# First attention with a constant guard and scores issued ahead of the transposes; expert weights read eight slots later

## The reference

```python
x = x + L0_xattn(layernorm(x), ctx, ctx, mask, Wq, bq, Wk, bk, Wv, bv)   # softmax attention over 257 rows
x = x + L0_attn(layernorm(x), ...)                                       # time mix and channel mix
x = x + L0_ffn(layernorm(x), Wg, We, be)                                 # 8 experts, top 2
x = x + L1_xattn(layernorm(x), ctx, wq, wk, wv, wo, ...)                 # quantised linear layers on ctx
x = x + L1_attn(layernorm(x), ...)                                       # state-space scan
x = x + L1_ffn(layernorm(x), gate_w, ..., w1, b1, w2, b2)                # 8 experts, top 1
```

```python
xn = ctx * rsqrt(mean(square(ctx), -1) + 1e-6)
scale = 127.0 / maximum(max(abs(xn), -1), 1e-5)
xq = round(xn * scale)
```

## Time and profile before

| | |
|---|---|
| median of 3 runs | 2150.19 us (2148.49 to 2154.41) |
| the profiled execution's own time | 2157.34 us |
| its span, first to last instruction | 2155.6 us |
| PE busy | 1442.8 us, 67% |
| DVE busy | 1382.0 us, 64% |
| ACT busy | 988.5 us, 46% |
| POOL busy | 750.6 us, 35% |
| mean granted TensorE clock | 0.773 of full speed |
| loop of the first attention | about 104 to 272 us of the span |
| the last two blocks | about 1380 us to the end |

### The profile page before, as it was taken

How to read it: one execution, slowest core, us unless ns; L and a number is a source line. 1 busy time by engine, 2 the same in 40 slices (tenths; PEclk the granted TensorE clock), 3 DMA queues, 4 the chain that set the end, 5 groups by cost and what they waited for, 6 DMA issues and landing times. The chain is left out here.

```text
span 2155.6 us, 34484 instructions
## 1 busy us (share of the span) xinstructions
PE 1442.8 (67%) x12500; PEld 798.0 (37%) x12500; DVE 1382.0 (64%) x2466; ACT 988.5 (46%) x1792; POOL 750.6 (35%) x804
## 2 busy tenths in 40 slices
PE   5578833336766498148888359344539879879998
PEld 3334412224544343025655133100114434434666
DVE  1267677773334676837777774399899889889110
ACT  2288722222111253225556233433339868868454
POOL 0034300000000532133344000056568688688543
PEclk8556666667888599569899579655659989989999
DMA  1245300001001053265564123599656546534000
GB/s 69 107 181 209 136 20 0 0 0 44 0 0 37 2 194 135 46 117 90 95 102 77 29 79 110 124 231 225 161 115 151 127 98 154 130 88 108 1 11 10
DMA packets 147472, 194.81 MB, mean 90 GB/s; under 512 B 106527, under 2 KB 111583, under 8 KB 134272
## 3 DMA queue, kind: packets, MB, share of 16 engines
q1 hardware_dynamic: 147332, 192.92, 35.4%
HBM read 146.46 MB, written 23.36 MB: 79 GB/s over the span
## 5 line engine op out<-in xcount | busy, mean ns | idle before, releaser
L2453 POOL TENSOR_TENSOR mf_st<-mf_st,mf_c_rep 128x1024 f32<-128x1024 f32 x128 | 300.9, 2351 | 348.4 <-DVE mf_st L2527 348.3
L2527 DVE TENSOR_TENSOR_SCAN mf_st<-mf_dA,mf_u_ps 128x512 f32<-128x512 f32 x256 | 310.4, 1213 | 0.0
L2355 PE MATMUL mf_y_ps<-mf_st,c_consts 128*32 128x512 f32 x512 | 155.8, 798 | 180.3 <-POOL mf_st L2453 133.4
L2638 ACT ACTIVATE mf_dA<-c_dt,c_neg_a 128x496 f32<-128x496 f32 x256 | 167.1, 701 | 116.1 <-DVE mf_st L2527 115.6
L2397 PE MATMUL mf_eh<-mf_parts,mf_w 128*128 128x512 f16 x768 | 198.1, 397 | 18.5 <-POOL mf_parts L2476 11.1
L2521 DVE TENSOR_TENSOR mf_u_ps<-mf_st,mf_b_ps 128x512 f32<-128x512 f32 x256 | 177.8, 695 | 25.7 <-DMA mf_st<-xs 14.7
L2417 PE MATMUL mf_ey<-mf_w,mf_hid 128*128 128x256 f16 x1536 | 192.9, 277 | 0.0
L2480 POOL TENSOR_TENSOR mf_hid<-mf_g,mf_hid 128x512 f16<-128x512 f32 x128 | 148.8, 1163 | 98.6 <-ACT mf_g L2655 98.5
L2417 PEld LDWEIGHTS mf_ey<-mf_w,mf_hid 128*128 128x128 f16 x1536 | 152.5, 99 | 49.9 <-issue 6.0
L1073 POOL TENSOR_SCALAR mg_we<-mg_we 128x2048 f32<-128x2048 f32 x2 | 10.8, 5395 | 432.3 <-DMA mg_we<-in_l_we 432.3
L2652 ACT ACTIVATE mf_hid<-mf_eh,c_vecs 128x512 f16<-128x512 f32 x128 | 88.0, 687 | 112.6 <-PE mf_eh L2397 112.1
(11 more groups left out here) (476 smaller groups left out, 2944.0 us busy)
## 6 DMA issues: line engine op xcount, KB each, us to landing
mf_st<-xs SPq DMA_DIRECT2D x64, 1024.0 KB, 7.2
a_ctx_t<-in_ctx_t SPq DMA_DIRECT2D x16, 1024.0 KB, 6.6
a_ctx_n<-in_ctx_n SPq DMA_DIRECT2D x16, 1024.0 KB, 4.9
mo_raw<-in_l_w SPq DMA_DIRECT2D x16, 512.0 KB, 3.7
ws<-mo_split SPq DMA_DIRECT2D x32, 256.0 KB, 2.4
mf_w<-ws SPq DMA_DIRECT2D x32, 256.0 KB, 14.6
xs<-mi_xc SPq DMA_DIRECT2D x16, 256.0 KB, 4.1
zs<-mi_sz SPq DMA_DIRECT2D x4, 1024.0 KB, 6.8
```

Of the source, the lines that this page charges most:

```text
L2355: m = e.matmul(y_ps[T * j:T * j + T, :], c.pick[:, gg, :], st[u % RING][:, j, :], start=(gg == 0), stop=(gg == 3))
L2453: e.tensor_tensor(half(u, h), half(u, h), over(c_rep[u // UNITS % 2][:, :], [P, 2, BT], 1), ALU.mult).then_inc(hcs("done"), 1)
L2527: e.tensor_tensor_scan(st[u % RING][:, j, :], dA[:, n % AHEAD, :], u_ps[j % 2][:, :], 0.0, ALU.mult, ALU.add).then_inc(hs("done"), 1)
L2638: e.activation(by_batch(dA[:, n % AHEAD, :])[:, :, 1:], dt, ACT.Exp, scale=c.neg_a[:, at:at + 1]).then_inc(dAs("done"), 1)
```

## The change

In the first attention the guard under the maximum becomes the constant `LEAST` in place of the root of the mean square: `roots` is gone with its two activations, the squares add straight into `c.c_ss` and the maxima are written straight to `c.c_max`, so that both copies go. On PE `score(t+1)` now stands ahead of `turn(t)`. In the last two blocks the expert matrices are read in slots 8 to 23.

```diff
+LEAST = 1e-5 * RMS_EPS ** 0.5
...
-        scale = Steps(sem("scale"), ["keep_max", "keep_ss", "guard", "flip", "scale"], 2)
+        scale = Steps(sem("scale"), ["guard", "flip", "scale"], 2)
...
             def turns(t, u, n):
-                turn(t, u)
                 if not last(t):
                     score(t + 1, 1 - u, n + u)
+                turn(t, u)
                 if not first(t):
                     turn_out(t - 1, 1 - u)
                 weigh(t, u, n)
...
-                e.tensor_reduce(qs[u][:, :], ctx_n[u][:, :, :, :].rearrange("p b k c -> p (b k) c"), AX.X, ALU.max,
+                e.tensor_reduce(c.c_max[:, bass.ds(t * 2 * BPT, 2 * BPT)], ctx_n[u][:, :, :, :].rearrange("p b k c -> p (b k) c"), AX.X, ALU.max,
                                 apply_absolute_value=True).then_inc(absmax("done"), 1)
...
                 e.wait_ge(*absmax.at("done", t))
-                e.tensor_copy(c.c_max[:, bass.ds(t * 2 * BPT, 2 * BPT)], qs[u][:, :]).then_inc(scale("keep_max"), 1)
-                e.wait_ge(*root_s.at("root", t))
-                e.tensor_copy(c.c_ss[:, bass.ds(t * 2 * BPT, 2 * BPT)], ss[u][:, :]).then_inc(scale("keep_ss"), 1)
-                e.wait_ge(*scale.at("keep_ss", t))
-                e.tensor_tensor(qs[u][:, :], qs[u][:, :], root[u][:, :], ALU.max).then_inc(scale("guard"), 1)
+                e.wait_ge(*roundings.at("done", t - 2))
+                e.tensor_scalar(qs[u][:, :], c.c_max[:, bass.ds(t * 2 * BPT, 2 * BPT)], LEAST, None, ALU.max).then_inc(scale("guard"), 1)
...
                 e.wait_ge(n_loaded[u], n * 16)
-                e.wait_ge(*scale.at("keep_ss", t - 2))
                 for r in range(2 * BPT):
                     e.wait_ge(*(squares.at("done", t, r - 1) if r else squares.at("done", t - 1)))
                     e.activation(sq[:, :], ctx_n[u][:, r // 2, r % 2, :], ACT.Square,
-                                 accum_out=ss[u][:, r:r + 1]).then_inc(squares("done"), 1)
-
-            def roots(t, u):
-                e.wait_ge(*squares.at("done", t))
-                e.wait_ge(*scale.at("guard", t - 2))
-                e.activation(root[u][:, :], ss[u][:, :], ACT.Ln, scale=1.0 / C,
-                             bias=c.eps[:, 1:2]).then_inc(root_s("log"), 1)
-                e.wait_ge(*root_s.at("log", t))
-                e.activation(root[u][:, :], root[u][:, :], ACT.Exp, scale=0.5,
-                             bias=c.eps[:, 2:3]).then_inc(root_s("root"), 1)
+                                 accum_out=c.c_ss[:, bass.ds(t * 2 * BPT + r, 1)]).then_inc(squares("done"), 1)
...
                 if not last(t):
                     exponentials(t + 1, 1 - u)
-                    roots(t + 1, 1 - u)
...
             for s in range(SLOTS):
                 b, p = post(s)
-                if s < 2 * E:
-                    fetch_weight(s)
+                if 8 <= s < 8 + 2 * E:
+                    fetch_weight(s - 8)
```

More of the change, by code:

```diff
@@ L408, in l0_attention @@
         qs = [sb(f"qs{u}", [P, 8]) for u in range(2)]
-        ss = [sb(f"ss{u}", [P, 8]) for u in range(2)]
-        root = [sb(f"root{u}", [P, 8]) for u in range(2)]
         s_ps = [ps(f"s_ps{u}") for u in range(2)]
@@ L424, in l0_attention @@
         absmax, outs, whole, added = step("absmax"), step("outs"), step("whole"), step("added")
-        scale = Steps(sem("scale"), ["keep_max", "keep_ss", "guard", "flip", "scale"], 2)
+        scale = Steps(sem("scale"), ["guard", "flip", "scale"], 2)
         exp, squares, kept, ot_kept = step("exp"), step("squares", 2 * BPT), step("kept", 2), step("ot_kept")
-        root_s = Steps(sem("root"), ["log", "root"], 2)
         scores, turned, summed, ot_turned, projected = (step(k) for k in ("scores", "turned", "summed", "ot_turned", "projected"))
@@ L690, in turns @@
                     exponentials(t + 1, 1 - u)
-                    roots(t + 1, 1 - u)
-            for each in (exp, squares, kept, ot_kept, root_s):
+            for each in (exp, squares, kept, ot_kept):
                 each.start(e)
@@ L696, in _ @@
             square(0, 0, 1)
-            roots(0, 0)
             over_tiles(e, turns)
```

## The result

The changed kernel takes 2173.08 us (median of 4 runs, 2170.76 to 2176.39) against 2149.34 us for the kernel before in the same comparison: a ratio of 1.0092, interval 1.0069 to 1.0115. It is slower. The forecast had the direction and the mechanism of the loss, but not its size: 9.8 us where 20 (by the ratio) to 24 (by the medians) were measured. The median lies 3 us above the top of the stated range; by the ratio, 2150.2 times 1.0092, it would be at 2170.0, the edge of it. The profiled execution of the changed kernel took 2172.14 us, with a span of 2170.6.

What follows compares the result with a forecast made beforehand. The prediction took PE's own 10.34 us a tile at 1.2 GHz as the first attention's bound, and DVE's input waits in the last blocks as removable. 2150.2 + 18.0 - 8.2 gave 2160.0 us, range 2139 to 2170.

Steps and rivals of the forecast that it cites:

- The order on PE: First attention: moving score(t+2) into the turn-to-turn chain lengthens tiles, so the last turn comes 18.0 us later.
- The chain of 9.14 + 2.74 = 11.88 us a tile: First attention, turn to turn: copy, squares, keep_out and projection take 9.14 us; the score, now behind the projection, adds 2.74.
- The idle gap ahead of L536: First attention: PE idles 1.5 us a tile before the projection, waiting for ACT's copy of the turned output.
- The addresses of the squares: ACT, first attention: run-time addresses for eight squares cost 0, hidden behind the square ahead; 0.6 us a tile for the range.
- the signs of being wrong: L536 following L521 without gap, 1.00 clock in the loop, squares over 4.19 us, or DVE input waits in slots 8-23.
- The clock: PE, first attention: the new gap ahead of every projection keeps the clock at 1.2 GHz throughout.
- the rival with fast spells: First attention: fast clock stays about every third tile, four spells save 8.4 us, total 2151.6 us; chance 0.12.
- The roots: ACT, first attention: removing 3.2 us a tile gains 0 in the loop; only tile 0's keep_turned starts earlier, 108.3 for 111.4.
- The expert weights: Last two blocks: reading expert matrices later removes all four DVE input waits, -8.2 us, bounds -3.9 and -8.2.
- The transfer rival: Last two blocks: transfers starve later, DVE waits there instead, 4.3 to 8.2 us come back, up to 2168 us; chance 0.12.
- The sum: Whole kernel: +18.0 for the first attention and -8.2 for the expert matrices give +9.8 us.

## Why the prediction was right or wrong, point by point

**The order on PE: right, mechanism and size.** The chain of 9.14 + 2.74 = 11.88 us a tile came out at 11.88 in the kernel with the order alone and in the one with fixed addresses. The idle gap ahead of L536 is there, 1.06 or 1.29 us with the order alone and 1.70 or 1.93 with the longer squares; I had 1.5. With the order alone PE also waits 0.58 or 0.28 us ahead of `weigh` for the copy of the turned probabilities, a wait that I had left out; the two together are 1.64 or 1.57, the forecast gap in two pieces.

**The addresses of the squares: the mis-sized term.** I took 0 and kept 0.6 us a tile as a bound, reasoning that ACT's sequencer does the register work while the square ahead runs. In this kernel it doesn't. One line of the changed kernel over two us, instructions with length min/median/max in ns, first and last start:

```profile
L656 ACTq FUSED_REGOPS  x3: 46/46/46, 131.7 to 132.9; - x3
```

The square that started at 131.15 has its sum read out from 131.46 to 131.65, the register operation starts at 131.7, the next square at 131.77. Each square waits for the one ahead, and the address is worked out behind that wait. The squares of tiles 0 and 1 have no such operation, those of the 14 tiles in the loop have one each, 112 in all. Squares start 0.62 to 0.63 us apart instead of 0.52 to 0.54; eight and the copy behind them come 0.63 later a tile, and because they lie on the chain all of it counts: 12.52 - 11.88 = 0.64. Over 14 tiles that is 8.8 to 9.0 us, in time 9.7 between the medians. With it the attention's loss would have been 18.0 + 8.8 = 26.8, and 26.7 was read, counted from the first exponential. Eight squares of more than 4.19 us stood among the signs of being wrong. The bound for the range was the right size, 0.6, but I had added it up as 2170 where 2160.0 + 8 is 2168.

**The clock: right.** No rise in the loop, 0.50 throughout, so the rival with fast spells in the changed kernel is out. The reason that I gave, the gap ahead of the projection, is argued and not shown. Once the gap was taken away, the clock was 0.68 and 0.77 over the stretch, but tiles without the gap ran at 0.50 as well.

**The roots: right that they were off the path**, and right at tile 0. With the guard alone the 3.4 us won there were lost again by tiles 0.3 us longer (last turn 1 us later); the longer squares are the likely cause, which no run shows by itself. In the changed kernel `keep_turned(0)` started at 109.64; less the 1.5 us by which the whole attention began later that is 108.2, where 108.3 was forecast. The Trainium skill's drain of 1.38 us behind a table load (ScalarE: Activation LUTs, "What ACT_TABLE_LOAD costs") is not to be seen: in before the load at 238.24 ends at 239.52, and its activation starts at 239.54. The guard alone says nothing of it, since the loads that it takes out were off the path.

In the kernels with the copy ahead of the squares the roots come to count, it seems, but the two ratios do not settle it.

**The expert weights: right in the waits and about right in the size.** All four waits went, none came in slots 8 to 23. I booked 8.2 us; alone the edit gave 5.8 (1.9 to 9.7), and the stage is 7.5 shorter over all profiles. The transfer rival was wrong for one matrix a slot and true for two.

**The sum.** In the profiled executions: the last turn +28.1, from there to the first weight product of the next block +2.4 (in before the clock rose behind the last turn and the last projection took half its time, in the changed kernel it did not; the prediction had put this at nothing), the middle blocks, which are unchanged, -4.2, and the last two -11.3, together the +15.0 between the spans. The medians differ by 23.7. So one profiled pair is uncertain by several us in stages that nobody touched. The 9.8 of the forecast missed some 9 to 10 for the addresses, 2.4 behind the last turn and under 1 for the weights; 9.8 + 9.7 + 2.4 + 0.7 = 22.6, between the 20 and the 24 that were measured.

## What to carry to other kernels

Before an instruction is moved ahead on an in-order engine, write down the chain of releases from that engine back to itself and see whether the moved work lands inside it; PE had 10.34 us of its own work and a chain of 9.14 beside it, so 2.74 us moved across were enough to turn the bound. A term that is put at nothing because it is hidden needs the same care as one that is on the path, once the path runs through it. The cure was on another engine: a short copy that releases the busiest engine belongs ahead of long work that nobody waits for. An address made at run time was not free here on an instruction that waits for its forerunner, since the register work started behind the wait.

## What the runs showed of the hardware that I had not expected

One FUSED_REGOPS of 46 ns, together with what stands around it, spaced dependent ACT instructions with an accumulator 0.08 to 0.10 us further apart. And unchanged stages moved by several us from one profiled execution to the next, 4.2 us less here between the first product of the second block and the first slot of the last, so that medians of a few runs are needed for anything under 0.3%.
